# A decoder layer on one core: the mask of the first four heads leaves TensorE for VectorE and GpSimd

## The reference

```python
x = x + _L0_xattn_ref(_layernorm(x), ctx_1024, ctx_1024, mask, wq, wk, wv, w_out)

scores = jnp.einsum('bhqd,bhkd->bhqk', Q, K) / np.sqrt(hd)          # 16 heads of width 16
scores = jnp.where(mask[:, None, :, :] == 1, -1000000000.0, scores)
attn = jax.nn.softmax(scores, axis=-1)
out = jnp.einsum('bhqk,bhkd->bhqd', attn, V)
```

## Time and profile before

| | |
|---|---|
| profiled execution, its own time | 1457.25 us |
| its span, first to last instruction | 1455.4 us |
| outside the span | 1.85 us |
| busy: PE, DVE, ACT, POOL | 1300.1, 906.3, 654.5, 522.8 us |
| mean granted TensorE clock | 0.952 of full speed |
| mask matmuls (L1121) | 384, 12 in each row |
| VectorE's head maxima (L2142) | 512, mean 542 ns |
| exponentials (L1624) | 384, mean 545 ns |

### The profile page before, as it was taken

The page is one execution under the profiler, slowest core; times in us unless marked ns, Lnnn a source line. Parts: engine busy times, 40 slices in busy tenths (PEclk is TensorE's granted clock), DMA queues, the critical chain, the costliest instruction groups (busy, mean ns, idle before and its releaser), DMA issues. The chain is left out here.

```text
span 1455.4 us, 34511 instructions
## 1 busy us (share of the span) xinstructions
PE 1300.1 (89%) x11121; PEld 1171.7 (81%) x11121; DVE 906.3 (62%) x2926; ACT 654.5 (45%) x1526; POOL 522.8 (36%) x716
## 2 busy tenths in 40 slices
PE   5999999999987599999999999999999876888976
PEld 4888988988987578888888888888888775777865
DVE  4676476576564466777666777667767474444546
ACT  3543433433423144555555555555555643444531
POOL 3233133133124313433444334443343651233344
PEclk9999999999988888999999999999999988999987
DMA  8699200000002264656556565566653332222367
GB/s 188 140 232 244 69 0 0 0 0 0 0 21 61 52 158 105 134 134 132 119 118 137 132 141 120 114 131 132 142 139 92 86 109 66 81 85 86 102 163 194
DMA packets 134974, 151.39 MB, mean 104 GB/s; under 512 B 41235, under 2 KB 118404, under 8 KB 134868
## 3 DMA queue, kind: packets, MB, share of 16 engines
q1 hardware_dynamic: 128148, 134.55, 40.1%
q0 software_dynamic: 6160, 15.69, 3.4%
q10 hardware_dynamic: 576, 0.07, 0.0%
HBM read 79.27 MB, written 45.82 MB: 86 GB/s over the span
## 5 line engine op out<-in xcount | busy, mean ns | idle before, releaser
L2142 DVE CUSTOM_DVE_ANT_0 junk<-psum,biasq 112x375 f32<-112x375 f32 x512 | 270.8, 542 | 152.4 <-issue 104.6
L1624 ACT ACTIVATE pr<-psum 125x448 f32<-125x448 f32 x384 | 205.5, 545 | 93.0 <-PE psum L1126 87.9
L1126 PE MATMUL psum<-qst,kst 97*125 97x224 f32 x768 | 226.6, 356 | 0.0
L1106 PE MATMUL psum<-kst,qst 96*112 96x376 f32 x512 | 187.9, 381 | 27.1 <-DMA qst<-qlo 19.4
L1126 PEld LDWEIGHTS psum<-qst,kst 97*125 97x125 f32 x768 | 147.9, 193 | 7.2 <-issue 0.2
L1121 PE MATMUL psum<-flagk,negbig 125*125 125x448 bf16 x384 | 140.0, 364 | 0.0
L1106 PEld LDWEIGHTS psum<-kst,qst 96*112 96x112 f32 x512 | 89.5, 180 | 56.7 <-DVE smax L2142 28.0
L700 POOL TENSOR_TENSOR rs<-rs,neg_half 112x1 f32<-112x1 f32 x32 | 18.2, 570 | 322.0 <-DVE rs L2055 319.9
L829 POOL DMA_INDIRECT routed_y<-yb,yrow x61 | 59.1, 968 | 138.5 <-ACT yb L1795 132.8
L1140 PE MATMUL psum<-pr,vaug 125*32 125x112 f32 x3072 | 95.1, 265 | 0.0
L1140 PEld LDWEIGHTS psum<-pr,vaug 125*32 125x32 f32 x3072 | 71.4, 111 | 15.9 <-issue 11.4
(11 more groups left out here) (306 smaller groups left out, 3544.0 us busy)
## 6 DMA issues: line engine op xcount, KB each, us to landing
kst<-khi SPq DMA_DIRECT2D x64, 376.0 KB, 6.8
routed_h<-in_route_pad SPq DMA_DIRECT2D x6, 3640.0 KB
kst<-klo SPq DMA_DIRECT2D x32, 376.0 KB, 9.5
ctxT<-in_ctxT SPq DMA_DIRECT2D x32, 375.0 KB, 6.2
hblk<-routed_h SPq DMA_DIRECT2D x61, 130.0 KB, 2.1
qst<-qhi SPq DMA_DIRECT2D x128, 56.0 KB, 4.5
stage<-in_e SPq DMA_DIRECT2D x21, 256.0 KB, 3.2
maskq<-in_mask SPq DMA_DIRECT2D x32, 164.1 KB
```

The lines of the kernel that those rows point to most:

```text
L1106: pe.matmul(bank[max_bank(n, hd)][0:T, 0:S2E], head(qst[par][0:ROWS], hd), pair(kst[par][0:ROWS], hd // 2), start=True, stop=True).then_in ...
L1126: mm = pe.matmul(bank[q % 3][0:KP, cols(i, 2 * T)], pair(kst[par], n)[:, cols(q // HPB, KP)], both(qst[par], n), start=False, stop=True, s ...
L1624: nc.scalar.activation(pr[q % PROBS][:].rearrange("k i q -> k (i q)"), bank[q % 3][0:KP, 0:GT], ACT.Exp, scale=1.0 / HD ** 0.5).then_inc(s ...
L2142: nc.vector.tensor_tensor_reduce(out=junk[:, hd % 2, :], in0=bank[max_bank(n, hd)][0:T, 0:S2], in1=biasq[:, par, :], scale=1.0, scalar=-3e ...
```

## The change

The mask term leaves TensorE in three of the twelve slots of a row, 0, 4 and 8, which are the first four heads in each third of the keys. There the first score matmul starts the bank instead. GpSimd makes a keep mask `keepk` from `flagk` once a row: 1 where a key counts, and 2^-100 where it doesn't. VectorE takes the exponentials of such a slot, cuts them at 2.0 and multiplies them by the keep mask, in place in `pr`, before `weighted_values` reads them. That is one instruction on GpSimd and three on VectorE in each row. The counters `tri0a` and `root_b` of the first stage are used again for it.

```diff
@@ gpsimd
+            def keep_keys(t, par):
+                b = t * RB + par
+                if not is_row(b, 0):
+                    wait_apart(pool, s["tri0a"], G + KC * b)
+                wait_apart(pool, s2["flags"], b + 1)
+                nc.gpsimd.tensor_scalar(keepk[:], flagk[:, par], 0.5, TINY, ALU.is_lt, ALU.max).then_inc(s["root_b"], 1)
+
             def step(t, par, masks=True, power=True):
+                keep_keys(t, par)
@@
             low_shared(1)
+            keep_keys(ROUNDS + 1, 1)
             scatter(*ahead(ROUNDS + 1, 1, -4))
@@ tensor, mask_scores
                 pe.wait_ge(s2["exp"], SLOTS * b + q + 1)
+                if q % HPB == 0:
+                    return
@@ tensor, score
-                mm = pe.matmul(..., start=False, stop=True, skip_group_check=True)
+                mm = pe.matmul(..., start=q % HPB == 0, stop=True, skip_group_check=True)
@@ tensor, weighted_values
                 pe.wait_ge(s2["exp"], SLOTS * b + q + 4)
+                if q % HPB == 0:
+                    pe.wait_ge(s["tri0a"], G + KC * b + c3 + 1)
@@ vector
+            def keep_values(t, par, q):
+                b = t * RB + par
+                c = q // HPB
+                if q == 0:
+                    dve.wait_ge(s["root_b"], G + b + 1)
+                dve.wait_ge(s2["exp"], SLOTS * b + q + 4)
+                kept = keepk[:, c, :].unsqueeze(1).broadcast_to([KP, HPB, T])
+                nc.vector.scalar_tensor_tensor(out=pr[q % PROBS][:], in0=pr[q % PROBS][:], scalar=2.0, in1=kept, op0=ALU.min, op1=ALU.mult).then_inc(s["tri0a"], 1)
@@ vector, step
                             low_k(*far, 1)
+                        if place == 2 and q in (3, 7):
+                            keep_values(t, par, (q - 3))
@@
                     scale_row(*coming)
+                keep_values(t, par, 2 * HPB)
+                if norm:
                     low_context(*coming)
```

More of the change, by code:

```diff
@@ L75 @@
 BIG = float(2 ** 40)
+TINY = float(2.0 ** -100)
 PAIRS = HEADS // 2
@@ L146, in decoder_layer @@
         stage = sb("stage", [P, STAGES, DC, EW])
+        keepk = sb("keepk", [KP, KC, T], BF16)
         stats = sb("stats", [T, GB, 6])
@@ L1125, in score @@
                 n = HPB // 2 * (q % HPB) + i
-                mm = pe.matmul(bank[q % 3][0:KP, cols(i, 2 * T)], pair(kst[par], n)[:, cols(q // HPB, KP)], both(qst[par], n), start=False, stop=True, skip_group_check=True)
+                mm = pe.matmul(bank[q % 3][0:KP, cols(i, 2 * T)], pair(kst[par], n)[:, cols(q // HPB, KP)], both(qst[par], n), start=q % HPB == 0, stop=True, skip_group_check=True)
                 if i == HPB // 2 - 1:
```

## The result

The changed kernel takes **1522.71 us** (median of 4 runs, 1521.85 to 1535.68), the kernel before 1456.92 (4 runs, 1454.64 to 1459.02) in the same comparison. The ratio is 1.0474 [1.0424, 1.0524]: 66 us slower. The execution that was profiled is the longest of them, 1535.68 us, and its trace shows more of the clock's falls than the others had (mean clock 0.926 against 0.930 and 0.931).

A forecast was written before the change was run, and what follows sets the result against it. A two-row round trip through GpSimd and the DMA queue was taken as the bound; 31.9 (trips) + 8 (clock) + 2 (ends) = 42 us on 1457.25 gave 1499, forecast 1500 us, range 1470 to 1526.

The forecast's parts named there:

- likeliest case: The change lengthens the two-row round trip, with clock falls on top: 1474 to 1520 us, 67 in 100.
- the last rival: VectorE's slot 3 instruction meets GpSimd's L695 and L696: +13 us, with clock falls 1520 to 1535, 7 in 100.
- The closed trip: Two-row loop through TensorE, VectorE, GpSimd's flags and the DMA queue sets the pace: 40.14 us.
- Both rivals on the faster side: TensorE's freed time wins: 1439, 8 in 100. Keep mask hidden, VectorE's part not: 1467 to 1477, 13 in 100.
- Slots 0, 3 and 7: Trip up to L700: mask matmul gone -0.20 us, VectorE's first two instructions +0.45 and +0.50.
- The end of the step on GpSimd: VectorE's third instruction, right before `low_context`, holds up GpSimd's `decide`: +0.50 us a trip, bounds 0 and 0.9.
- whoever comes first: Port rule for VectorE and GpSimd: the one that takes the shared SBUF ports first keeps them to its instruction's end.
- `keep_keys`: GpSimd's keep mask ahead of L695 and L696: 1.2 us plus 0.1 for waits, +1.30 a trip, bounds 0.9 and 1.5.
- 12.5 trips: Round trips in 25 rows, each 2.55 us longer: 31.9 us.
- the term "+2": First five or six rows gain nothing net, last two may lose 1 to 3 us on GpSimd: together +2 us.
- half of the 12.5 trips: TensorE's clock falls after long waits at a step's start, counted for half the trips: 8 us, bounds 0 and 16.
- Each one fills the idle time that causes it: A clock fall uses up TensorE's wait before the first maximum, so only half the trips were counted: 8 us.

The follow-up runs named there:

- 28 us alone: Kernel before plus GpSimd's keep mask, made but used by nobody; all mask matmuls stay: 1488.24 us, ratio 1.0217.
- nine dummies: Changed kernel with nine matmuls of no use ahead of heads 0 and 1 of each step: 1506.73 us, ratio 1.0301.
- the masks dropped alone: Kernel before without the mask matmuls of slots 0, 4 and 8, nothing in their place: 1465.58 us, ratio 1.0025.
- moving VectorE's part: Changed kernel with VectorE's second instruction moved from slot 7 to slot 5 and its third behind `low_context`: 1522.72 us, ratio 1.0442.
- VectorE's part moved as well: Changed kernel with GpSimd's order flags, keep mask, scatters, and VectorE's second instruction in slot 5, third behind `low_context`: 1446.49 us, ratio 0.9936.

## Why the prediction was right, and which terms were off

The direction and the mechanism were right: 1522.71 lies in the range, near its upper end, 23 us above the 1500 forecast. That it still lies in the range is in part luck. The likeliest case's own 1474 to 1520 was just passed, and its high bounds (41, 16 and 2 us on 1457.75) add up to 1517 only. The range reached 1526 because of the last rival, whose 1520 to 1535 holds the measured time and whose mechanism didn't occur (below).

**The closed trip** is shown, not only argued. The flags 2.95 us earlier, with no work removed, give 1.8%, and TensorE's 19 us removed, of which only slot 0's 0.20 us a row lie on the trip, give nothing measurable. Both rivals on the faster side fall with these two: TensorE's time doesn't come free, and the keep mask isn't hidden (28 us alone).

**The trip's length.** The kernel with nine dummies is the clean reading. Its trip is 16.83 + 11.83 + 13.93 + 0.52 = 43.1 us; forecast were 40.14 + 2.55 = 42.7. A little of it may be the dummies' own, since from the landing to the start it is 0.52 where it was 0.30. Term by term:

- Slots 0, 3 and 7: -0.20 + 0.45 + 0.50 put L702 at 16.82 after the start, measured 16.83. Mean against mean the growth is smaller, 16.83 - 16.22 = +0.61 instead of +0.75. VectorE's instruction has a median of 619 ns (0.62 was forecast) and in slot 3 the next maximum starts 0.53 us after it began:

```profile
793.37 0.62 DVE L2167 SCALAR_TENSOR_TENSOR pr<-pr,keepk 125x448 f32<-125x448 f32 x1
793.90 0.54 DVE L2157 CUSTOM_DVE_ANT_0 junk<-psum,biasq 112x375 f32<-112x375 f32 x1
...
803.36 0.62 DVE L2167 SCALAR_TENSOR_TENSOR pr<-pr,keepk 125x448 f32<-125x448 f32 x1
803.90 0.93 DVE L1925 TENSOR_TENSOR clo<-ctxT,chi 128x750 fp32r<-128x750 f32 x1
```

- The end of the step on GpSimd: from L702 to the end of L733 it is 806.92 - 801.87 = 5.05 us, where it was 4.31: +0.74 instead of +0.50. L721 is the long one, 1.72 us, and L728 (once L726) took 0.31. The mechanism is as forecast: VectorE's third instruction starts at 803.36, `low_context` (L1925) ends at 804.83, and L721 stands from 803.22 to 804.94, through both. By these records L721 began 0.14 us before VectorE's instruction and was still the one held up, so "whoever comes first" can't be read from the starts here.
- `keep_keys`: 1.36 us instead of 1.2, but from the end of L733 to that of L698 it is 813.58 - 806.92 = 6.66 against 5.54, +1.12 instead of +1.30. One of the waits ahead of the scatter is met while `keepk` is made. The two errors cancel: +1.86 against +1.80, and on the mean +1.88 (11.83 - 9.95).
- 12.5 trips, 25 rows, were to cost 31.9 us. Over the 22 rows from row 6 to row 28 the kernel with nine dummies took 475.4 us and the one before 441.1, +34.3, which is 3.1 us a trip instead of 2.55; per 25 rows that would be 39. So this term was 7 us too small.

**Ends: the term "+2" was mis-sized.** That kernel's span is 47.5 us longer (1502.9 and 1455.4): 34.3 in these rows, 4.6 ahead of row 6 and 8.6 behind row 28. So the stretches outside the 22 rows hold 13 us. Counted as the forecast was, 25 rows and the rest, it is 39 and 8.5 us instead of 31.9 and 2. "No chain of this kind binds" in the first rows doesn't fit the 4.6 us lost there, and the last rows cost more than the "1 to 3 us" put down to GpSimd's tight queue. No experiment took the ends apart, so which instruction there costs it stays open.

**The clock: "half of the 12.5 trips", 8 us, was at most half of it.** In the timed runs the changed kernel is 16 us above the one with nine dummies (1522.71 - 1506.73), the upper bound I gave; by the ratios, as the two were timed in different comparisons, it is 25. The dummies may hold up a start themselves, so these are rough figures. In the profiled execution it is 31 us more than with nine dummies (78.5 us over the span of before, against 47.5). Three parts of that step failed:

- The price of a fall. I took +1.27 from one fall of 3.4 us after 1.71 us of idle time. In 590 to 1150 the changed kernel has thirteen falls of 3.4 to 10.2 us, six of them the longest, and an odd row, which carries them, takes 19.71 us to L702, 2.9 more than with nine dummies and 1.7 more than the 18 forecast.
- The shape of the idle time. I spread it evenly, 2.1 us a row, "in nearly every row". It gathers, 3.8 us, in every second row.
- "Each one fills the idle time that causes it." The rows at 781.45 and 804.35 show what happens instead. The low clock makes the odd row long, so that the even row starts 1.81 us after its landing and waits for nothing; the even trip has slack. But the late L702 is part of the odd trip itself, and its next start, at 827.78, has again waited 3.77 us. A fall delays the very chain whose lateness caused it, and keeps itself going. This reading is argued from these rows. What is shown is that removing the idle time removes both the falls and the alternation.

**The other forecasts.** Busy share 0.89 (about 0.90), row 22.8 us (21 to 22; 21.6 without falls), L702 to flags 11.87 (11.4 to 12), flags to start 14.45 without falls (13.5 to 14.3, slightly above). VectorE's slot 3 didn't meet L697 and L698: its instruction has a median of 619 ns and a maximum of 911 in 96, so that rival plays no part, although the time lies in its 1520 to 1535.

**Left open.** How often the clock falls differs between executions of one program (0.926 to 0.931 of mean clock in the changed kernel, with up to 14 us between them), and nothing here says why. Nor is it settled why the masks dropped alone bring more falls, or why moving VectorE's part won nothing in the timed runs when its trip was shorter. With the falls as large as the terms, differences of 10 us between kernels that have them can't be given to one instruction.

## What to carry to other kernels

Where an engine is 96% busy and still waits a little in each iteration, look for the chain that closes over several iterations through the slow engines and a DMA queue, and add up its parts before removing work. Here moving two short instructions of an idle engine ahead of two scatters gave 26 us, and taking 19 us of matmuls from the busiest engine gave none. An instruction added to such a chain costs its length in every trip, and once the wait it makes lowers TensorE's clock, more on top, here 16 to 25 us on 41 to 50; and after mending one loop, read the waits again, since the next (the scatters' landing) may be right behind it.

## What the runs showed of the hardware

- TensorE's clock fell in a gap of 3.45 us and was at 0.50 for the nine us behind it, where a wait of 1.71 us had brought 3.4 us of it. The length of the gap alone doesn't tell that of the fall: a gap of 4.04 us, from 734.1, was followed by 3.4 us. Inside the closed loop the falls cost 16 to 25 us, by the kernel with nine dummy matmuls a row (2.17 us), which held the clock at 1.00 in 590 to 1150. Six left 27 us at 0.50, and twelve cost what they saved.
- A VectorE instruction of the kind `scalar_tensor_tensor` holds GpSimd up as `low_context` does. When the two follow each other GpSimd doesn't get in between: L721 took 1.72 us, and with their order turned round L726 took 1.52.
- GpSimd makes 125 x 336 bf16 elements with two operations in 1.36 us from bf16, and with one operation in 1.06 from int32.
- A scatter issued 1.7 us after the instruction that sets off a burst on the other queue landed 8.4 to 9.0 us after it was issued in full, while the DMA engines were 0.97 and 0.95 busy. In the kernel with VectorE's part moved as well, behind the same order on GpSimd, the engines were 0.90 and 0.94 busy, and nobody waited for the scatters.
